# A GRU after a causal convolution on one core: the prologue's order of issue, and step 0's n part in a PSUM bank of its own

## The chip, the cores and the metric

The kernel runs on one core of a Trainium2 chip. The metric is the device time of one execution in microseconds (us), as the median of several runs. A profile is one further execution, whose span runs from its first to its last instruction.

## The reference

The input x has 16 rows (batch), 256 time steps and 512 channels; cond has 16 rows of 512. First a causal convolution over time with 16 taps in each channel, whose weights are the rows of cond, is added to x. Then a GRU cell runs over the 256 steps from the state h = cond, and its states are added to x.

```python
x = x + conv(x, w=cond_2048[:, None, :])     # depthwise, 16 taps, left padding of 15
def cell(h, x):
    gi = x @ W_ih + b_ih                     # [16, 1536]
    gh = h @ W_hh + b_hh
    i_r, i_z, i_n = split(gi, 3); h_r, h_z, h_n = split(gh, 3)
    r = sigmoid(i_r + h_r); z = sigmoid(i_z + h_z)
    n = tanh(i_n + r * h_n)
    return (1 - z) * n + z * h
x = x + scan(cell, h0=cond_2048, inputs=x)
```

All of it is in float32. The 256 steps depend on each other.

## The kernel before

The 512 channels lie as C = 4 chunks (c) of 128 on the partitions. A step is worked in H = 2 halves (f), each with two chunks of the output. A half's pre-activations stand in a PSUM bank `pg[m % 3][f]`, where m = t // 2 since a bank holds two steps at once; its 512 columns are split into the n part of the recurrence (columns 0 to 128), r and z (128 to 384) and the n part of the input (384 to 512). ScalarE first seeds a bank with the biases (`seed`, L430). Then TensorE adds the input's product (`product(q)`, L301: m, f and c are digits of q, and one q is four matmuls of 192 columns) and the recurrence's (`recur(t, f, c)`, L325, also four matmuls of 192). Every float32 matmul of these is two rows in the trace, so one `recur` or `product` is 8 rows, and a step is 64 rows of `recur` and 32 of `product`. The products of a step's round are for a later m; they are what TensorE does while the other engines turn the gates into the new state.

That chain runs once for each half: VectorE transposes r and z out of PSUM (L539) and n beside it (L543), ScalarE makes r and z (L461) and 1 - z (L463), VectorE scans n (L551), ScalarE takes the tanh (L466), GpSimd has z*h ready (L290), and VectorE scans the new h (L564). TensorE's next step waits for `s_h[0]`, and for `s_h[1]` after 24 of its rows.

Ahead of step 1 stands a **prologue**, written by hand and separately for each engine:

- SyncE queues the loads in one row: cnd (cond), xs (the first 16 steps of x), the four chunks of W_ih, the four of W_hh (`whh[:, c, F:]`, 768 KB each, L229). Then it waits for the third chunk of W_hh, loads `xb[1]`, and goes on with small loads (`tz`, `xw`) for the convolution of steps 16 to 47 on TensorE (`turn`, in steps 4, 6 and 9).
- ScalarE queues the two biases and, once GpSimd has made `cpad`, the store of the taps. It makes 16 diagonal matrices from cond (L446), seeds six banks, moves chunk 3 of x out of `pcv[0]` (L451), loads the table of the sigmoid (L452), and copies the n columns of each chunk of W_hh to the front of its row when the chunk has come (L455, 630 ns each). `recur` reads n, r and z as one strip of 192 columns, which needs that copy.
- TensorE zeroes the six banks of `pg` (L370), runs WARM = 6 matmuls on zeros (L372), the taps of chunk 3 (L364), the 16 products of m = 0 and 1, then step 0: chunk by chunk of W_hh, each with its wait, and with IDLE matmuls on zeros behind chunks 0 and 1. The last chunk is done by `recur_first` (L334), in matmuls of 128 and 64 columns, without the copy. Four products of m = 2 follow.
- VectorE copies cond into h, makes the biases (`bc`), then the convolution of chunks 0 to 2 for the first 16 steps: `first` and 48 pieces of `rest`. Before the last LATE = 22 of them stand the two transposes of the input's n part (`transpose_in`), for which step 0 waits.

## Time and profile before

| what | us |
|---|---|
| median of 3 runs | 1025.57 |
| lowest and highest | 1025.18, 1025.68 |
| the profiled execution | 1025.25 |
| its span | 1023.5 |
| TensorE busy with matmuls | 1015.4 |
| step 1's first matmul | 24.81 |
| from one step to the next, in steady state | 3.90 |

In the timeline rows the columns are start, time from the first start to the last end, engine, line, operation, tiles, shapes and count; in brackets the idle time of the engine before it and what ended it. PEld is TensorE's load of weights, ACTq and SPq the issue of DMAs. Most of the span is 255 steps of the same shape; the change touches what lies ahead of step 2.

### The profile page before, as it was taken

To read this page: it belongs to the slowest core of one execution; us is meant where nothing else is said; L and a number is where in the kernel's file an instruction comes from. 1 tells how busy PE (TensorE), PEld (TensorE's weight loads), DVE (VectorE), ACT (ScalarE), POOL (GpSimd) and SP (SyncE) were. 2 spreads that over 40 slices of the span, in tenths; PEclk is the share of its full clock that TensorE was granted. 3 is DMA by queue.
4 is the path that set the end of the run, shared out by engine and by line. 5 is a ranking of instruction groups with operands and counts; after the bars stand their busy time and mean duration, and the time that the engine had idled before them with its cause. 6 is when DMAs were issued, how large, how long until landed. Compare 5 with 4: busy or idle time off the path is not lost.

```text
span 1023.5 us, 58209 instructions
## 1 busy us (share of the span) xinstructions
PE 1015.4 (99%) x24837; PEld 902.6 (88%) x24838; DVE 865.1 (85%) x2851; ACT 399.3 (39%) x1816; POOL 237.4 (23%) x784
## 2 busy tenths in 40 slices
PE   8999999999999999999999999999999999999997
PEld 6988888888888888899999999999999999999986
DVE  7788888888888888888888888888888887777555
ACT  5334333333433343333434333343433333343333
POOL 3222222222222222222222222222222222222222
PEclk9999999999999999999999999999999999999999
DMA  8721001010100101001010010101001000000000
GB/s 297 73 34 39 19 21 30 15 36 19 29 25 12 34 19 34 23 12 35 15 39 19 15 36 11 39 19 29 22 14 35 14 29 16 11 29 4 24 14 12
DMA packets 66450, 32.07 MB, mean 31 GB/s; under 512 B 43920, under 2 KB 65040, under 8 KB 66192
## 3 DMA queue, kind: packets, MB, share of 16 engines
q1 hardware_dynamic: 65760, 28.25, 10.7%
q8 instruction: 195, 3.19, 1.3%
q14 instruction: 63, 0.52, 0.2%
q10 hardware_dynamic: 432, 0.11, 0.0%
HBM read 19.86 MB, written 8.49 MB: 28 GB/s over the span
## 4 chain that ended last, share of the span: by engine, by line
PE 97%; issue 1%; POOL 1%; DVE 0%; DMA 0%; ACT 0%; POOLq 0%; DVEq 0%
PE pg L328 65%; PE pg L318 32%; POOL tz L277 1%; PE pcv L356 0%; DMA cnd<-cond 0%; DVE hp L564 0%; POOL nzh L290 0%; DVE gt L539 0%; DVE gn L543 0%; ACT rz L461 0%; POOL cpad L267 0%; POOL nzh L274 0%; POOL rz L272 0%; POOL zcp L273 0%; POOL cpad L269 0%
## 5 line engine op out<-in xcount | busy, mean ns | idle before, releaser
L328 PE MATMUL pg<-whh,hp 128*32 128x192 f32 x16368 | 716.8, 326 | 2.1 <-ACT whh L455 1.1
L328 PEld LDWEIGHTS pg<-whh,hp 128*32 128x32 f32 x16368 | 594.3, 110 | 74.8 <-DVE hp L564 2.7
L318 PE MATMUL pg<-wih,x 128*32 128x192 f32 x8192 | 385.4, 326 | 0.0
L290 POOL TENSOR_TENSOR nzh<-rz,hp 128x32 f32<-128x32 f32 x512 | 158.0, 309 | 780.0 <-ACT rz L461 780.0
L318 PEld LDWEIGHTS pg<-wih,x 128*32 128x32 f32 x8192 | 296.5, 110 | 35.0
L461 ACT ACTIVATE rz<-gt 128x64 f32<-128x64 f32 x512 | 136.1, 266 | 484.6 <-DVE gt L539 459.1
L506 DVE SCALAR_TENSOR_TENSOR x<-xb,cnd,x 128x512 f32<-128x512 f32 (+1 forms) x420 | 294.6, 702 | 8.0
L564 DVE TENSOR_TENSOR_SCAN hp<-zcp,nzh 128x96 f32<-128x96 f32 x512 | 173.0, 338 | 41.4 <-ACT nzh L466 40.7
L539 DVE STREAM_TRANSPOSE gt<-pg 128x128 f32<-128x128 f32 x512 | 160.2, 313 | 50.8 <-PE pg L328 42.6
L551 DVE TENSOR_TENSOR_SCAN an<-rz,gn 128x64 f32<-128x64 f32 x512 | 148.7, 290 | 52.2 <-ACT rz L461 52.0
L466 ACT ACTIVATE nzh<-an 128x32 f32<-128x32 f32 x512 | 120.8, 236 | 125.6 <-DVE an L551 125.6
L463 ACT ACTIVATE zcp<-gt 128x32 f32<-128x32 f32 x512 | 111.0, 217 | 0.0
L543 DVE STREAM_TRANSPOSE gn<-pg 128x64 f32<-128x64 f32 x512 | 106.5, 208 | 0.0
L437 ACT ACTIVATE pg<-bc 128x256 f32<-128x256 f32 x256 | 86.4, 370 | 0.0
L284 POOL TENSOR_TENSOR x<-x,hp 128x64 f32<-128x64 f32 x255 | 81.5, 320 | 0.0
L534 DVE STREAM_TRANSPOSE gn<-pg 128x64 f32<-128x64 f32 x256 | 57.7, 226 | 0.1
L506 DVE SCALAR_TENSOR_TENSOR x<-xb,cnd 128x512 f32<-128x512 f32 (+1 forms) x28 | 19.3, 688 | 0.0
L490 DVE SCALAR_TENSOR_TENSOR x<-xs,cnd,x 128x192 f32<-128x192 f32 (+11 forms) x45 | 11.6, 335 | 0.0
L517 DVE SCALAR_TENSOR_TENSOR x<-xb,cnd,x 128x512 f32<-128x512 f32 x15 | 10.9, 727 | 0.2
L277 POOL MEMSET tz<- 128x2048 f32 x3 | 5.3, 1805 | 1.0 <-DVE bc L585 1.0
L455 ACT ACTIVATE whh<-whh 128x512 f32<-128x512 f32 x4 | 2.5, 630 | 7.1 <-DMA whh<-w_hh 7.1
L356 PEld LDWEIGHTS pcv<-tz,xw 128*32 128x32 f32 x192 | 5.0, 110 | 0.3
(47 smaller groups left out, 49.4 us busy)
## 6 DMA issues: line engine op xcount, KB each, us to landing
xb<-x SPq DMA_DIRECT2D x96, 94.0 KB, 2.0
out<-x SPq DMA_DIRECT2D x60, 128.0 KB, 1.9
wih<-w_ih SPq DMA_DIRECT2D x4, 768.0 KB, 8.0
whh<-w_hh SPq DMA_DIRECT2D x4, 768.0 KB, 14.2
xw<-x SPq DMA_DIRECT2D x24, 64.0 KB, 3.3
xb<-x SPq DMA_DIRECT2D x16, 62.0 KB, 1.8
tz<-taps SPq DMA_DIRECT2D x12, 64.0 KB, 3.5
xs<-x SPq DMA_DIRECT2D x1, 512.0 KB, 4.6
```

The lines of the kernel that those rows point to most:

```text
L290: pool.tensor_tensor(nzh[:, f, ::2, :, 1], chunks(rz[:, f, 1, :, 1]), h_of(t - 1, slice(f * CH, (f + 1) * CH)), ALU.mult).then_inc(s_zh[f], 1)
L318: i = pe.matmul(pg[m % Q][f][D * j:D * (j + 1), RZ:END], x1_of(c, 2 * m, 2 * m + 2), wih[:, c, :, :].rearrange("p (g k) (j d) -> p j g k d ...
L328: i = pe.matmul(pg[t // 2 % Q][f][D * j:D * (j + 1), 0:IN], hp[:, t % 2, 2 * c + 1 - t % 2:2 * c + 3 - t % 2, :, 1].rearrange("p u b -> p ...
L437: act.activation(pg[m % Q][f][:, 0:END], bc[:, f, :], ACT.Copy).then_inc(s_seed[f], 1)
L461: act.activation(rz[:, f, :, :, 1].rearrange("p g (c b) -> p (g c) b", b=B), gt[:, f, :, u], ACT.Sigmoid).then_inc(s_rz[f], 1)
L463: act.activation(zcp[:, f, ::2, :, 1], gt[:, f, CH:, u], ACT.Sigmoid, scale=-1.0).then_inc(s_zc[f], 1)
L466: act.activation(nzh[:, f, ::2, :, 0], chunks(an[:, f, :, 1]), ACT.Tanh).then_inc(s_n[f], 1)
L506: dve.scalar_tensor_tensor(o, xx[:, c, (K - 1 - lag) * B:(K - 1 - lag + n) * B], cnd[:, c, K - 1 - lag:K - lag], o if lag else now, ALU.mu ...
L539: dve.transpose(gt[:, f, :, :].rearrange("p c r -> p (c r)"), pg[t // 2 % Q][f][:, RZ:IN]).then_inc(s_trz[f], 1)
L543: dve.transpose(gn[:, t // 2 % 2, :, f, :, :, 0].rearrange("p u c b -> p c u b"), pg[t // 2 % Q][f][:, 0:RZ]).then_inc(s_tn[f], 1)
L551: dve.tensor_tensor_scan(an[:, f].rearrange("p n s -> p (n s)"), rz[:, f, 0].rearrange("p n s -> p (n s)"), gn[:, t // 2 % 2, t % 2, f].re ...
L564: dve.tensor_tensor_scan(hp[:, (t + 1) % 2, a:a + n].rearrange("p c b s -> p (c b s)"), zcp[:, f, 0:n].rearrange("p c b s -> p (c b s)"), ...
```

## The change

Step 0's recurrence for n goes to the bank `pcv[1]`, both halves side by side (`recur_n`), and r and z alone to `pg[0][f]` (`recur_rz`). So no chunk of step 0 needs ScalarE's copy, and the last chunk of W_hh is loaded in two DMAs, the r and z columns (512 KB, semaphore s_whh[3]) and then the n columns (256 KB, s_whl). ScalarE seeds `pcv[1]` with the biases (two activations of 128 columns), and TensorE zeroes one bank more. VectorE's `transpose_n` of step 0 waits for the new semaphore s_gn, which the last `recur_n` raises for both halves.

Order: cond is loaded by ScalarE's queue as its third DMA, no longer by SyncE's as its first. The sigmoid's table is loaded ahead of the diagonals by an activation on zeros. The store of the taps stands behind the fourth diagonal. On VectorE the biases come ahead of cond's copies, and LATE is 18. GpSimd's four memsets come ahead of its work on cond. Of the hunks left out below, one moves GpSimd's memsets and one VectorE's copies of cond; the others declare semaphores, or count the new waits. Three products of m = 2 are moved in between the chunks of W_hh, the chunk c = 3 of each half first, and step 0 has five instead of four, step 1 three instead of four. IDLE is 3 behind chunk 0 and 4 behind chunk 1.

```diff
@@ -30,8 +30,8 @@
 TAPS = 3 * K
 FEW = 4
 WARM = 6
-LATE = 22
-IDLE = {0: 5, 1: 3}
+LATE = 18
+IDLE = {0: 3, 1: 4}
 M2 = T // 2
 RZ, IN, END = CH * D, 3 * CH * D, 4 * CH * D
 Q = 3
...
@@ -154,7 +157,7 @@
             def until(t):
                 n = C * (t + 1) if t <= THIN else C * (THIN + 1) + (C - 1) * (t - THIN)
                 return 2 * H * C + min(n, H * C * (M2 - 2))
-            return range(until(t - 1), until(t))
+            return range(until(t - 1) + (t == 1), until(t))
 
         def inputs(t):
 
@@ -221,12 +224,13 @@
                 sp.wait_ge(s_o, b)
                 sp.dma_start(out[:, c, a * B:b * B], x1_of(c, a, b)).then_inc(s_out[k], 16)
 
-            sp.dma_start(cnd[:, :, :], cond).then_inc(s_cnd, 16)
             sp.dma_start(xs[:, :, :], x[:, :, 0:TB * B]).then_inc(s_xs, 16)
             for c in range(C):
                 sp.dma_start(wih[:, c, :, :], w_ih[:, c, :, :]).then_inc(s_wih[c], 16)
-            for c in range(C):
+            for c in range(C - 1):
                 sp.dma_start(whh[:, c, F:], w_hh[:, c, :]).then_inc(s_whh[c], 16)
+            sp.dma_start(whh[:, C - 1, F:3 * F], w_hh[:, C - 1, 0:2 * F]).then_inc(s_whh[C - 1], 16)
+            sp.dma_start(whh[:, C - 1, 3 * F:], w_hh[:, C - 1, 2 * F:]).then_inc(s_whl, 16)
             sp.wait_ge(s_whh[C - 2], 16)
             sp.dma_start(xb[1][:, 0, :], x[:, 0, B:(W2 + TB) * B]).then_inc(s_xe, 16)
             for t in range(T):
...
@@ -301,12 +305,15 @@
             def product(q):
 
                 m, f, c = q // (H * C), q // C % H, q % C
+                if m == 2:
+                    c = (c - 1) % C
                 if m < 2 and f == 0:
                     pe.wait_ge(s_wih[c], 16)
                 if m < 2 and c < C - 1:
                     pe.wait_ge(s_first, len(FIRST))
+                if q % C == 0:
+                    pe.wait_ge(s_seed[f], m + 1)
                 if c == 0:
-                    pe.wait_ge(s_seed[f], m + 1)
                     if FEW <= 2 * m < TB:
                         pe.wait_ge(s_first, len(FIRST) + len(REST))
                     elif TB <= 2 * m < LONG[0][0]:
@@ -319,7 +326,7 @@
                                   wih[:, c, :, :].rearrange("p (g k) (j d) -> p j g k d", g=3, j=J)
                                   [:, j, :, f * CH:(f + 1) * CH],
                                   start=False, stop=True, skip_group_check=True)
-                if c == C - 1:
+                if q % C == C - 1:
                     i.then_inc(s_gi[f], 1)
 
             def recur(t, f, c):
@@ -331,15 +338,20 @@
                                   start=False, stop=True, skip_group_check=True)
                 return i
 
-            def recur_first(f, c):
-
-                hh = hp[:, 0, 2 * c + 1:2 * c + 3, :, 1].rearrange("p u b -> p (u b)")
+            def recur_rz(f, c):
+
                 for j in range(J):
-                    o = pg[0][f][D * j:D * (j + 1), :]
-                    pe.matmul(o[:, RZ:IN], hh,
-                              whh[:, c, F:3 * F].rearrange("p (g j f n) -> p j f g n", g=2, j=J, f=H)[:, j, f],
-                              start=False, stop=True, skip_group_check=True)
-                    i = pe.matmul(o[:, 0:RZ], hh,
+                    i = pe.matmul(pg[0][f][D * j:D * (j + 1), RZ:IN],
+                                  hp[:, 0, 2 * c + 1:2 * c + 3, :, 1].rearrange("p u b -> p (u b)"),
+                                  whh[:, c, F:3 * F].rearrange("p (g j f n) -> p j f g n", g=2, j=J, f=H)[:, j, f],
+                                  start=False, stop=True, skip_group_check=True)
+                return i
+
+            def recur_n(f, c):
+
+                for j in range(J):
+                    i = pe.matmul(pcv[1][D * j:D * (j + 1), f * RZ:(f + 1) * RZ],
+                                  hp[:, 0, 2 * c + 1:2 * c + 3, :, 1].rearrange("p u b -> p (u b)"),
                                   whh[:, c, 3 * F:].rearrange("p (j f n) -> p j f n", j=J, f=H)[:, j, f],
                                   start=False, stop=True, skip_group_check=True)
                 return i
@@ -368,6 +380,7 @@
             for q in range(Q):
                 for f in range(H):
                     pe.matmul(pg[q][f][:, :], zeros[:, 0:P], zeros[:, :], start=True, stop=True).then_inc(s_bits, 1)
+            pe.matmul(pcv[1][:, :], zeros[:, 0:P], zeros[:, :], start=True, stop=True).then_inc(s_bits, 1)
             for _ in range(WARM):
                 pe.matmul(pcv[0][:, :], zeros[:, 0:P], zeros[:, :], start=True, stop=True)
             pe.wait_ge(s_xs, 16)
@@ -387,19 +400,25 @@
             pe.wait_ge(s_tin[1], 1)
             for f in range(H):
                 pe.wait_ge(s_h[f], 1)
-            for c in range(C):
+            pe.wait_ge(s_seed_n, H)
+            for c in range(C - 1):
                 pe.wait_ge(s_whh[c], 16)
-                if c < C - 1:
-                    pe.wait_ge(s_whn, c + 1)
                 for f in range(H):
-                    if c < C - 1:
-                        recur(0, f, c)
-                    else:
-                        recur_first(f, c).then_inc(s_gh[f], 1)
+                    recur_rz(f, c)
+                    recur_n(f, c)
+                if c < H:
+                    product((2 * H + c) * C)
                 for _ in range(IDLE.get(c, 0)):
                     pe.matmul(pcv[0][:, :], zeros[:, 0:P], zeros[:, :], start=True, stop=True)
-            for q in products(0):
-                product(q)
+            product(2 * H * C + 1)
+            pe.wait_ge(s_whh[C - 1], 16)
+            for f in range(H):
+                recur_rz(f, C - 1).then_inc(s_gh[f], 1)
+            pe.wait_ge(s_whl, 16)
+            recur_n(0, C - 1)
+            recur_n(1, C - 1).then_inc(s_gn, 1)
+            for c in range(1, C - 1):
+                product(2 * H * C + c + 1)
             pe.wait_ge(s_whn, C)
             for t in range(1, T):
                 m = t // 2
...
@@ -438,20 +457,25 @@
 
             act.dma_start(bih[:, :], b_ih).then_inc(s_small, 16)
             act.dma_start(bhh[:, :], b_hh).then_inc(s_small, 16)
-            act.wait_ge(s_cp, 3)
-            act.dma_start(scratch[:, :, :], cpad[:, :, :]).then_inc(s_scr, 16)
+            act.dma_start(cnd[:, :, :], cond).then_inc(s_cnd, 16)
+            act.wait_ge(s_clear, 1)
+            act.activation(pre[:, :], zeros[:, 0:B], ACT.Sigmoid)
             act.wait_ge(s_eye, 2)
             act.wait_ge(s_cnd, 16)
             for lag in range(K):
+                if lag == J:
+                    act.wait_ge(s_cp, 3)
+                    act.dma_start(scratch[:, :, :], cpad[:, :, :]).then_inc(s_scr, 16)
                 act.activation(diagonal(lag), eye[:, :], ACT.Copy, scale=cnd[:, C - 1, K - 1 - lag:K - lag]).then_inc(s_dg, 1)
             for m in range(Q):
                 for f in range(H):
                     seed(m, f)
+            for f in range(H):
+                act.activation(pcv[1][:, f * RZ:(f + 1) * RZ], bc[:, f, 0:RZ], ACT.Copy).then_inc(s_seed_n, 1)
             act.wait_ge(s_c3, 1)
             act.activation(x1[:, C - 1, 0:TB * B], pcv[0][:, 0:TB * B], ACT.Copy).then_inc(s_ev, 1)
-            act.activation(pre[:, :], cnd[:, 0, :], ACT.Sigmoid)
             for c in range(C):
-                act.wait_ge(s_whh[c], 16)
+                act.wait_ge(s_whh[c] if c < C - 1 else s_whl, 16)
                 act.activation(whh[:, c, 0:F], whh[:, c, 3 * F:], ACT.Copy).then_inc(s_whn, 1)
             act.wait_ge(s_zero, 4)
             for t in range(T):
@@ -540,8 +564,11 @@
                               pg[t // 2 % Q][f][:, RZ:IN]).then_inc(s_trz[f], 1)
 
             def transpose_n(t, f):
+                if t == 0:
+                    dve.wait_ge(s_gn, 1)
+                g = pg[t // 2 % Q][f][:, 0:RZ] if t else pcv[1][:, f * RZ:(f + 1) * RZ]
                 dve.transpose(gn[:, t // 2 % 2, :, f, :, :, 0].rearrange("p u c b -> p c u b"),
-                              pg[t // 2 % Q][f][:, 0:RZ]).then_inc(s_tn[f], 1)
+                              g).then_inc(s_tn[f], 1)
 
             def scan_n(t, f):
 
...
```

On TensorE, from the end of the 16 products (pg10, pg11) to step 1, this stood before (`s_whn` is ScalarE's copy, L318 a product, L400 an idle matmul):

```order
L328 MATMUL pg00<-whh,hp 32x192 [waits s_h1,s_whh0,s_h0,s_whn,s_tin1,s_tin0]
L328 MATMUL pg00<-whh,hp 32x192 x3
L328 MATMUL pg01<-whh,hp 32x192 x4
L400 MATMUL pcv0<-zeros 128x512 x5
L328 MATMUL pg00<-whh,hp 32x192 [waits s_whn,s_whh1]
L328 MATMUL pg00<-whh,hp 32x192 x3
L328 MATMUL pg01<-whh,hp 32x192 x4
L400 MATMUL pcv0<-zeros 128x512 x3
L328 MATMUL pg00<-whh,hp 32x192 [waits s_whn,s_whh2]
L328 MATMUL pg00<-whh,hp 32x192 x3
```

Now, from the chunk c = 2 on (L344 is r and z, L353 n, L325 a product, L412 an idle matmul):

```order
L344 MATMUL pg00<-whh,hp 32x128 [waits s_whh2]
L344 MATMUL pg00<-whh,hp 32x128 x3
L353 MATMUL pcv1<-whh,hp 32x64 x4
L344 MATMUL pg01<-whh,hp 32x128 x4
L353 MATMUL pcv1<-whh,hp 32x64 x4
L325 MATMUL pg20<-wih,x1 32x192 [waits s_first]
L325 MATMUL pg20<-wih,x1 32x192 x3
L344 MATMUL pg00<-whh,hp 32x128 [waits s_whh3]
L344 MATMUL pg00<-whh,hp 32x128 x3
L344 MATMUL pg01<-whh,hp 32x128 x4
L353 MATMUL pcv1<-whh,hp 32x64 [waits s_whl]
L353 MATMUL pcv1<-whh,hp 32x64 x7
```

The recurrence for n has left the bank of r and z, twice as many matmuls stand in each chunk, no wait for the copy is left, and a product has come ahead of the last chunk's wait. Two more stand ahead of this piece, behind the chunks c = 0 and 1.

On ScalarE, from the start to the first copy of W_hh, before:

```order
L439 DMA bih<-b_ih 128x12
L440 DMA bhh<-b_hh 128x12
L442 DMA taps<-cpad 128x192 [waits s_cp]
L446 ACT_TABLE_LOAD [waits s_cnd]
L446 ACTIVATE xb<-eye,cnd 128x128 [waits s_eye]
L446 ACTIVATE xb<-eye,cnd 128x128 x15
L437 ACTIVATE pg<-bc 128x256 [waits s_bc,s_bits] x6
L451 ACTIVATE x<-pcv 128x256 [waits s_c3]
L452 ACT_TABLE_LOAD
L452 ACTIVATE pre<-cnd 128x16
L455 ACTIVATE whh<-whh 128x512 [waits s_whh0]
```

and now:

```order
L458 DMA bih<-b_ih 128x12
L459 DMA bhh<-b_hh 128x12
L460 DMA cnd<-cond 128x64
L462 ACT_TABLE_LOAD
L462 ACTIVATE pre<-zeros 128x16 [waits s_clear]
L469 ACTIVATE xb<-eye,cnd 128x128 [waits s_cnd,s_eye]
L469 ACTIVATE xb<-eye,cnd 128x128 x3
L468 DMA taps<-cpad 128x192 [waits s_cp]
L469 ACTIVATE xb<-eye,cnd 128x128 x12
L456 ACTIVATE pg<-bc 128x256 [waits s_bc,s_bits] x6
L474 ACTIVATE pcv<-bc 128x64 x2
L476 ACTIVATE x<-pcv 128x256 [waits s_c3]
L479 ACTIVATE whh<-whh 128x512 [waits s_whh0]
```

One of the two table loads is gone, the other stands ahead of the wait for cond, and cond's own load is third in this engine's queue.

On VectorE in step 0, now (L563 is r and z, L570 n, L578 the scan of n, L591 that of h):

```order
L563 STREAM_TRANSPOSE gt<-pg00 128x128 [waits s_gh0]
L570 STREAM_TRANSPOSE gn<-pcv1 128x2x2x16 [waits s_gn]
L578 SCALAR_TENSOR_TENSOR an<-rz,gn 128x64 [waits s_tin0,s_tn0,s_rz0]
L563 STREAM_TRANSPOSE gt<-pg01 128x128 [waits s_gh1]
L570 STREAM_TRANSPOSE gn<-pcv1 128x2x2x16 [waits s_gn]
L591 SCALAR_TENSOR_TENSOR hp<-zcp,nzh 128x96 [waits s_zc0,s_zh0,s_n0]
```

The rows are those of before but for the wait for s_gn, and for pcv1 as what n is read from.

## Rows read from the trace of the kernel before

**Rows 1.** The page: busy time of each engine; the instruction queue (packets, MB, share).

```profile
PE 1015.4 (99%) x24837; PEld 902.6 (88%) x24838; DVE 865.1 (85%) x2851; ACT 399.3 (39%) x1816; POOL 237.4 (23%) x784
...
q8 instruction: 195, 3.19, 1.3%
```

**Rows 2.** Timeline of TensorE from 3.79 us to step 3.

```profile
3.79 2.67 PE L372 MATMUL pcv<-zeros 128*128 128x512 bf16 x6
...
16.53 0.86 PE L328 MATMUL pg<-whh,hp 128*32 128x192 f32 x16
...
19.38 0.86 PE L328 MATMUL pg<-whh,hp 128*32 128x192 f32 x16 [0.80 <-ACT whh L455]
20.16 0.82 PE L400 MATMUL pcv<-zeros 128*128 128x512 bf16 x3
...
22.35 0.45 PE L339 MATMUL pg<-whh,hp 128*32 128x128 f32 x8
...
23.07 1.49 PE L318 MATMUL pg<-wih,x 128*32 128x192 f32 x31
24.81 2.81 PE L328 MATMUL pg<-whh,hp 128*32 128x192 f32 x64 [0.24 <-DVE hp L564]
27.40 1.51 PE L318 MATMUL pg<-wih,x 128*32 128x192 f32 x32
28.70 2.81 PE L328 MATMUL pg<-whh,hp 128*32 128x192 f32 x64
```

**Rows 3.** Timeline of ScalarE in the prologue.

```profile
3.65 1.28 ACT L446 ACT_TABLE_LOAD   x1 [3.65 <-POOL cpad L269]
4.94 4.79 ACT L446 ACTIVATE xb<-eye,cnd 128x128 f32<-128x128 f32 x16
...
20.48 0.63 ACT L455 ACTIVATE whh<-whh 128x512 f32<-128x512 f32 x1 [1.25 <-DMA whh<-w_hh]
22.33 0.63 ACT L455 ACTIVATE whh<-whh 128x512 f32<-128x512 f32 x1 [1.22 <-DMA whh<-w_hh]
23.42 0.26 ACT L461 ACTIVATE rz<-gt 128x64 f32<-128x64 f32 x1 [0.46 <-DVE gt L539]
```

**Rows 4.** Timeline of VectorE: the convolution's start, step 0, step 1's first h.

```profile
5.87 0.68 DVE L480 SCALAR_TENSOR_TENSOR x<-xs,cnd 128x64 f32<-128x64 f32 x3 [0.88 <-DMA xs<-x]
...
16.06 0.37 DVE L534 STREAM_TRANSPOSE gn<-pg 128x64 f32<-128x64 f32 x2
16.36 4.42 DVE L490 SCALAR_TENSOR_TENSOR x<-xs,cnd,x 128x128 f32<-128x128 f32 x22
...
23.71 0.29 DVE L551 TENSOR_TENSOR_SCAN an<-rz,gn 128x64 f32<-128x64 f32 x1 [0.26 <-ACT rz L461]
...
24.30 0.36 DVE L564 TENSOR_TENSOR_SCAN hp<-zcp,nzh 128x96 f32<-128x96 f32 x1
...
28.05 0.31 DVE L564 TENSOR_TENSOR_SCAN hp<-zcp,nzh 128x96 f32<-128x96 f32 x1
```

**Rows 5.** Timeline of SyncE's queue: the first two loads.

```profile
0.81 0.39 SPq L224 DMA_DIRECT2D cnd<-cond  x1
1.25 0.68 SPq L225 DMA_DIRECT2D xs<-x  x1
```

**Rows 6.** DMA issues: queue, count, KB each, median us to landing.

```profile
taps<-cpad ACTq DMA_DIRECT2D x1, 96.0 KB, 7.3
cnd<-cond SPq DMA_DIRECT2D x1, 32.0 KB, 1.8
```

**Rows 7.** Stretches of 1 us: start:end, length, each engine's busy time, PEclk, DMA share, GB/s.

```profile
19.00:20.00 1.00, 0.62 (x16) 0.50 (x16) 1.00 (x7) 0.23 (x1) 0.00 (x0) 1.00 1.03 420
20.00:21.00 1.00, 0.99 (x11) 0.21 (x3) 0.78 (x6) 0.52 (x1) 0.00 (x0) 1.00 0.44 178
```

**Rows 8.** DMA queues by stretch, 16.0:17.3, then 22.4:24.0: packets, MB, share of 16 engines.

```profile
q8 instruction: 1, 0.02, 4.6%
...
q8 instruction: 1, 0.02, 4.4%
```

More of the change, by code:

```diff
@@ L91, in build @@
         s_whh = [sem(f"s_whh{c}") for c in range(C)]
+        s_whl = sem("s_whl")
         s_whn = sem("s_whn")
@@ L114, in build @@
         s_x1 = sem("s_x1")
+        s_seed_n = sem("s_seed_n")
         s_seed = halves("s_seed")
@@ L117, in build @@
         s_tin = halves("s_tin")
+        s_gn = sem("s_gn")
         s_gh = halves("s_gh")
@@ L264, in _ @@
                                channel_multiplier=1).then_inc(s_eye, 1)
+            pool.memset(an[:, :, :, :], 0.0).then_inc(s_zero, 1)
+            pool.memset(rz[:, :, :, :, :], 0.0).then_inc(s_zero, 1)
+            pool.memset(zcp[:, :, :, :, :], 0.0).then_inc(s_zero, 1)
+            pool.memset(nzh[:, :, :, :, :], 0.0).then_inc(s_zero, 1)
             pool.wait_ge(s_cnd, 16)
@@ L270, in _ @@
                                ALU.add).then_inc(s_cp, 1)
-            pool.memset(an[:, :, :, :], 0.0).then_inc(s_zero, 1)
-            pool.memset(rz[:, :, :, :, :], 0.0).then_inc(s_zero, 1)
-            pool.memset(zcp[:, :, :, :, :], 0.0).then_inc(s_zero, 1)
-            pool.memset(nzh[:, :, :, :, :], 0.0).then_inc(s_zero, 1)
             pool.wait_ge(s_bc, H)
@@ L432, in seed @@
                 if m < Q:
-                    act.wait_ge(s_bits, 2 * Q)
+                    act.wait_ge(s_bits, 2 * Q + 1)
                     act.wait_ge(s_bc, H)
@@ L570, in _ @@
             dve.memset(hp[:, :, :, :, :], 0.0).then_inc(s_clear, 1)
-            dve.wait_ge(s_cnd, 16)
-            dve.wait_ge(s_clear, 2)
-            for f in range(H):
-                dve.tensor_copy(h_of(-1, slice(f * CH, (f + 1) * CH)),
-                                cnd[:, f * CH:(f + 1) * CH, :]).then_inc(s_h[f], 1)
             dve.wait_ge(s_small, 32)
@@ L587, in _ @@
                               ).then_inc(s_bc, 1)
+            dve.wait_ge(s_cnd, 16)
+            dve.wait_ge(s_clear, 2)
+            for f in range(H):
+                dve.tensor_copy(h_of(-1, slice(f * CH, (f + 1) * CH)),
+                                cnd[:, f * CH:(f + 1) * CH, :]).then_inc(s_h[f], 1)
             dve.wait_ge(s_xs, 16)
```

## The prediction

> **What bounds the kernel now.** The page first: TensorE is busy for 1015.4 of 1023.5 us [rows 1]. The timeline of TensorE shows where that comes from: step 1 starts at 24.81 and step 2 at 28.70, 3.89 us later, with no idle time between the 64 rows of the recurrence and the 32 of products [rows 2]. From step 1 almost to the end the time is a count of matmuls, and 255 steps times 3.9 us are there whatever the prologue does. Whatever moves step 1's start moves the end by as much, as long as no later step has to wait. So the question is what releases step 1, and the timelines of the other engines up to 24.81 answer it, read backwards. Step 1 waits for h: its scan ends at 24.30 + 0.36 = 24.66, and the matmul comes 0.15 later. That scan follows the scan of n at 23.71 by 0.59 [rows 4]. The scan of n waits for r at 23.42 + 0.26 = 23.68 on ScalarE [rows 3], r for VectorE's transpose and that for the last chunk of W_hh, whose matmuls start at 22.35 [rows 2]. They start with the landing: ScalarE's copy of the same chunk starts at 22.33, after an idle 1.22 that a DMA ended, and the copy of the chunk before at 20.48, likewise [rows 3]. The chain of the prologue is a stream of loads, then 2.48 us of work.
>
> **The loads.** SyncE issues cond at 0.81 and xs at 1.25 [rows 5]. With cond gone from its queue, xs and the eight weights behind it start 0.44 earlier. All 16 engines of the DMA are full up to 20 us (share 1.03) [rows 7], so the stream is bound by bytes, and the bytes are the same. I take 0.44 for the landings; the ends are 0 (the start was not what set them) and 0.44. The n columns, now the last load, then land at 22.33 - 0.44 = 21.89. The r and z columns are two thirds of a chunk that takes 22.33 - 20.48 = 1.85, so they land 0.62 before that, at 21.27.
>
> **The chain behind the last load.** ScalarE's copy of the last chunk still stands ahead of the first r, and it now waits for the n columns. It runs from 21.89 for 0.63 to 22.52 [rows 3]. TensorE and VectorE work beside it. The last chunk took TensorE 23.07 - 22.35 = 0.72 [rows 2]; r and z, two thirds, can be done from 21.27 on, and VectorE can transpose them before the copy ends. So r starts at the copy's end instead of 23.42: 22.54 to 22.80, and the scan of n 0.03 later at 22.83. The n part needs a third of 0.72 after 21.89, some 0.1 of latency, and a transpose of about 0.2, which ends at 22.45 and is hidden under the copy. Gain: 23.71 - 22.83 = 0.88, half of it from the stream, half from taking matmuls and a transpose out of the chain.
>
> **Is TensorE there in time?** Its path ahead of that is new. VectorE's transposes for step 0 started at 16.06, and LATE puts four more pieces ahead of them; the 22 that followed took 0.20 each, and the first are the longest [rows 4], so I take 0.25 each: 16.06 - 0.44 + 1.0 + 0.37 = 17.0. TensorE's own work ended at 16.53, and one more zeroing matmul costs (6.29 - 3.79) / 6 = 0.42, which gives 16.95, the same [rows 2]. From 17.0: three chunks of 0.72, three products of 8 rows (1.30 / 4 = 0.33 each), seven idle matmuls of 0.22 to 0.27 (three of them took 0.82 to the end of the last [rows 2]), at 0.22, make 4.7, so it reaches the r and z part of the last chunk at 21.7, 0.4 after it has landed. It is through at 21.7 + 0.72 = 22.4, and the scan of n could come at 22.8 by this path. The two paths are equal within the 0.2 us that I can't resolve; the copy's wait for TensorE in chunk 1, 0.80 idle [rows 2], is gone and has been filled with products. I count no loss, and 0.3 as the far end.
>
> **Step 1 has 24 rows of products.** That is 8 times 1.30 / 32 = 0.33 less [rows 2]. But step 2 waits for h, ready at 28.05 + 0.31 = 28.36 and usable 0.15 later, at 28.51, where it started at 28.70 [rows 2, 4]. The gain is 0.19, and the chain is late next; from step 2 on a step has 32 rows again and covers it. The bounds are 0 and 0.33. The product that left step 1 runs ahead of the last chunk, under the wait for loads.
>
> **At nothing.** The table load (1.28, from 3.65) and the diagonals behind it (4.79) [rows 3] are off the path: one load remains and runs before cond is there, the diagonals may start earlier, but TensorE takes them only from 6.7 on. ScalarE's two new seeds and the store of the taps lie in its pause before the first copy. SyncE's queue behind the weights moves earlier with them.
>
> **Sum.** 0.88 + 0.19 = 1.07 us. Against the profiled execution, 1025.25 - 1.07 = 1024.18; that execution is 0.32 under the median, so 1024.5 for the median.
>
> **Rival 1: a fetch of instructions lands on the last load.** The share of the DMA falls from 1.03 to 0.44 between 20 and 21 us, yet the last chunk lands only at 22.33 [rows 3, 7]. Most DMA engines are done and a few are late. Between 16.0 and 17.3 a packet of the instruction queue held 4.6% of 16 engines, 0.046 x 16 x 1.3 = 0.96 us of one engine, and the next came after 22.4, when the weights were in [rows 8]. TensorE's 24,837 matmuls and 24,838 loads of weights over 195 packets are 255 instructions to a packet [rows 1]. Behind the 16 products, 240 instructions led through the last product before; now the doubled matmuls and the moved products make 238 by the end of chunk 2, at about 21.2. So the second packet falls at about 21, with the last load still running. If it goes to the engine that is late already, n lands up to 0.96 later, at 22.85, the copy follows, and the scan of n comes at 23.79: 0.08 lost, 0.19 gained, 1025.45; half a hit gives 1025.0. Against it: no row says which engine fetches, and 0.4 us decide whether the packet still meets the load. The Trainium skill (Runtime: NRT & Kernel Launch, Instruction fetch mechanics) says that a sequencer refills in blocks of 256 instructions over its own DMA queue and that crossing a block is mostly hidden. The trace agrees on the size; by "mostly hidden" this rival would be nothing and the time 1024.5, and no row here tells what a block does to a load beside it.
>
> **Rival 2, the slower side: cond lands late.** It is now ScalarE's third DMA, behind xs and the first weights; with a DMA each 0.44, as SyncE's first two stand [rows 5], it is issued at 0.81 + 0.88 = 1.7. The nearest rows are cond alone, 1.8 us to landing, and the taps on the same queue among the weights, 7.3 us [rows 6]: it lands between 3.5 and 9.0. VectorE started its convolution at 5.87, when xs had come [rows 4]; that is 5.43 now, and with the two copies of h ahead (0.32) it needs cond by 5.1. Each microsecond beyond moves VectorE's convolution, hence its transposes, TensorE's step 0 and the end. At 6.15 the whole gain is gone; at 9.0 the loss is 3.9 - 1.07 = 2.83, and the time 1028.4. I take 4.2, near the cond row: it is a third of the taps' bytes, and it runs beside xs, where the taps met the full stream of weights. The Trainium skill (DMA: Bandwidth & Descriptors, Queues, rings and completion order) says that each DMA engine takes turns between its queues packet by packet; by that a short load does not stand behind the weights, which would give 1024.5 too. The 7.3 us of the taps show that taking turns can be slow.
>
> **How the numbers follow.** Forecast 0.46, 1024.5. Rival 1 0.33, 1025.0 to 1025.5. Rival 2 0.09, of which 0.04 beyond 8.2 us, where it costs more than 2 us. Waits that open in later steps, up to 0.5 us (SyncE's queue for the turns starts only 0.44 earlier, TensorE 1.07), 0.05. A larger gain than summed, by a stream that starts still earlier, 0.07. The range from 1023.9 to 1025.9 takes in the first, rival 1, the later waits and the mild part of rival 2; it leaves out about 0.13. A change of less than 0.2%, 2.05 us, is not told from none by a measurement of this kernel, and every likely case lies within: faster 0.03, same 0.93, slower 0.04.
>
> **What would show it.** Step 1's first matmul at 23.9, the scan of n at 22.8, ScalarE's last copy at 21.9, step 2 3.7 us after step 1. Rival 1: the last copy past 22.4 with r and z's matmuls near 21.7, and the instruction packet before 21.9. Rival 2: the diagonals start after 5.1. Later waits: idle time ahead of the turns in steps 4, 6 and 9. The forecast is wrong if ScalarE's last copy starts no earlier than 22.33, or if idle time opens in the steps behind.

## The result, and the profile after

| | before | after |
|---|---|---|
| median of 12 executions each, us | 1025.51 | 1027.78 |
| lowest to highest, us | 1025.18 to 1025.89 | 1027.60 to 1028.34 |
| profiled execution, us | 1025.25 | 1028.33 |
| its span, us | 1023.5 | 1026.6 |

The ratio of after to before is 1.0023, with a 95% interval of 1.0015 to 1.0030. The change made the kernel slower by 2.27 us; 1024.5 was forecast, and 1027.78 lies above the range. The profiled execution of after is 0.55 above its median, so the trace shows 3.08 us of difference where the medians show 2.27. Of the executions reported below, one ran at a granted clock of 0.56 from start to end and took 1803 us (the first of the kernel with six more matmuls ahead); it is left out, and its trace was not used.

The page of after: the busy time of TensorE, and the lines of the chain that ended last.

```profile
PE 1017.0 (99%) x24885; PEld 867.7 (85%) x24886; DVE 865.6 (84%) x2851; ACT 399.6 (39%) x1817; POOL 238.6 (23%) x784
...
PE pg L335 65%; PE pg L325 32%; DMA cnd<-cond 1%; PE pcv L376 1%; PE pcv L368 0%; PE pg L344 0%; PE pcv L412 0%; PE pcv L353 0%; DVE hp L591 0%; DVE gt L563 0%; DVE gn L570 0%; ACTq L459 0%; ACT xb L469 0%; ACTq L458 0%; POOL nzh L294 0%
```

The last line names what is new: the load of cond stands in the chain with 1% of 1026.6 us. The timelines show it. ScalarE in after (start, length, instruction, in brackets the idle time before it and what ended it), and the time from the issue of cond to its landing:

```profile
1.71 0.53 ACTq L460 DMA_DIRECT2D cnd<-cond  x1
...
8.71 0.69 ACT L469 ACTIVATE xb<-eye,cnd 128x128 f32<-128x128 f32 x2 [4.94 <-DMA cnd<-cond]
...
19.30 0.63 ACT L479 ACTIVATE whh<-whh 128x512 f32<-128x512 f32 x1 [1.27 <-DMA whh<-w_hh]
22.33 0.63 ACT L479 ACTIVATE whh<-whh 128x512 f32<-128x512 f32 x1 [2.39 <-DMA whh<-w_hh]
```
```profile
DMA to landing us min/median/max: 6.9/6.9/6.9
```

VectorE in after, from the copies of h to the transposes for step 0:

```profile
8.65 0.31 DVE L613 COPY hp<-cnd 128x32 f32<-128x32 f32 x2 [2.51 <-DMA cnd<-cond]
8.88 0.67 DVE L504 SCALAR_TENSOR_TENSOR x<-xs,cnd 128x64 f32<-128x64 f32 x3
...
20.06 0.46 DVE L558 STREAM_TRANSPOSE gn<-pg 128x64 f32<-128x64 f32 x2
```

TensorE in after, from the taps to step 2:

```profile
9.17 6.35 PE L376 MATMUL pcv<-xs,xb 128*128 128x256 f32 x32 [1.91 <-ACT xb L469]
15.44 5.41 PE L325 MATMUL pg<-wih,x 128*32 128x192 f32 x128
20.67 0.40 PE L344 MATMUL pg<-whh,hp 128*32 128x128 f32 x8
...
25.63 0.62 PE L344 MATMUL pg<-whh,hp 128*32 128x128 f32 x16
...
28.07 2.81 PE L335 MATMUL pg<-whh,hp 128*32 128x192 f32 x64 [0.95 <-DVE hp L591]
...
31.77 1.51 PE L335 MATMUL pg<-whh,hp 128*32 128x192 f32 x32
```

Read against before. The convolution starts 8.88 - 5.87 = 3.01 later [rows 4]. VectorE's transposes for step 0 start 20.06 - 16.06 = 4.00 later: those 3.01, and 1.0 for the four pieces put ahead of them. Step 1 starts 28.07 - 24.81 = 3.26 later, step 2 31.77 - 28.70 = 3.07 later [rows 2], and that is the whole difference of the spans, 3.1. Nothing is lost or won behind step 2. The last load of W_hh lands at 22.33, as in before [rows 3], but TensorE comes to the last chunk only at 25.63: in after the loads don't bound the prologue, cond does.

How TensorE took this: from 7.26 to 9.17 it had nothing to do, and the granted clock (the figure ahead of DMA share and GB/s) fell from its upper level, 2.4 GHz, to 1.2 GHz, and came back during the next stretch:

```profile
10.00:12.00 2.00, 2.00 (x7) 1.83 (x6) 2.00 (x11) 2.00 (x8) 2.00 (x2) 0.50 0.99 412
12.00:14.00 2.00, 2.00 (x12) 2.00 (x12) 2.00 (x7) 2.00 (x8) 2.00 (x2) 0.66 1.05 420
```

So there were two candidates for the loss beside each other, VectorE's late convolution and TensorE's slow taps, both behind one landing; and one question on the landing: why 6.9 us, where the same 32 KB took 1.8 in before [rows 6]?

### The profile page after: what moved, and what is told of

It reads as the page before. It is cut to its first block, busy times and chain, and to the rows that moved or that the text cites. A ratio compares the mean times of both kernels' runs of the same rounds, so it can differ in the third digit from the quotient of the medians.

```text
span 1026.6 us, 58303 instructions
## 1 busy us (share of the span) xinstructions
PE 1017.0 (99%) x24885; PEld 867.7 (85%) x24886; DVE 865.6 (84%) x2851; ACT 399.6 (39%) x1817; POOL 238.6 (23%) x784
## 4 chain that ended last, share of the span: by engine, by line
PE 98%; DMA 1%; DVE 0%; issue 0%; ACTq 0%; ACT 0%; POOL 0%; POOLq 0%; DVEq 0%
PE pg L335 65%; PE pg L325 32%; DMA cnd<-cond 1%; PE pcv L376 1%; PE pcv L368 0%; PE pg L344 0%; PE pcv L412 0%; PE pcv L353 0%; DVE hp L591 0%; DVE gt L563 0%; DVE gn L570 0%; ACTq L459 0%; ACT xb L469 0%; ACTq L458 0%; POOL nzh L294 0%
## 5 line engine op out<-in xcount | busy, mean ns | idle before, releaser
L335 PEld LDWEIGHTS pg<-whh,hp 128*32 128x32 f32 x16320 | 568.3, 110 | 97.6 <-DVE hp L591 2.8
L325 PE MATMUL pg<-wih,x 128*32 128x192 f32 x8192 | 384.4, 326 | 0.0
L325 PEld LDWEIGHTS pg<-wih,x 128*32 128x32 f32 x8192 | 284.1, 110 | 46.9
L591 DVE TENSOR_TENSOR_SCAN hp<-zcp,nzh 128x96 f32<-128x96 f32 x512 | 173.3, 339 | 41.8 <-ACT nzh L490 41.2
L563 DVE STREAM_TRANSPOSE gt<-pg 128x128 f32<-128x128 f32 x512 | 160.3, 313 | 49.9 <-PE pg L335 42.4
L578 DVE TENSOR_TENSOR_SCAN an<-rz,gn 128x64 f32<-128x64 f32 x512 | 149.4, 292 | 51.6 <-ACT rz L485 51.3
L570 DVE STREAM_TRANSPOSE gn<-pg 128x64 f32<-128x64 f32 x510 | 106.4, 209 | 0.0
L376 PE MATMUL pcv<-xs,xb 128*128 128x256 f32 (+15 forms) x32 | 6.3, 369 | 1.9 <-ACT xb L469 1.9
L376 PEld LDWEIGHTS pcv<-xs,xb 128*128 128x128 f32 x32 | 6.0, 237 | 2.5 <-ACT xb L469 2.3
L469 ACT ACTIVATE xb<-eye,cnd 128x128 f32<-128x128 f32 x16 | 4.8, 388 | 4.9 <-DMA cnd<-cond 4.9
```

The lines of the kernel that those rows point to most:

```text
L325: i = pe.matmul(pg[m % Q][f][D * j:D * (j + 1), RZ:END], x1_of(c, 2 * m, 2 * m + 2), wih[:, c, :, :].rearrange("p (g k) (j d) -> p j g k d ...
L335: i = pe.matmul(pg[t // 2 % Q][f][D * j:D * (j + 1), 0:IN], hp[:, t % 2, 2 * c + 1 - t % 2:2 * c + 3 - t % 2, :, 1].rearrange("p u b -> p ...
L563: dve.transpose(gt[:, f, :, :].rearrange("p c r -> p (c r)"), pg[t // 2 % Q][f][:, RZ:IN]).then_inc(s_trz[f], 1)
L570: dve.transpose(gn[:, t // 2 % 2, :, f, :, :, 0].rearrange("p u c b -> p c u b"), g).then_inc(s_tn[f], 1)
L578: dve.tensor_tensor_scan(an[:, f].rearrange("p n s -> p (n s)"), rz[:, f, 0].rearrange("p n s -> p (n s)"), gn[:, t // 2 % 2, t % 2, f].re ...
L591: dve.tensor_tensor_scan(hp[:, (t + 1) % 2, a:a + n].rearrange("p c b s -> p (c b s)"), zcp[:, f, 0:n].rearrange("p c b s -> p (c b s)"), ...
```

## The experiments

Theory: cond's late landing is the whole loss, and it is late because its packets take turns with SyncE's full queue. Rivals: the prologue's new order costs by itself (TensorE later at the last chunk, the instruction packet); the fallen clock sets the end; cond is late because of its place in ScalarE's own queue.

**cond back on SyncE's queue, the rest of the change kept.**

```diff
+            sp.dma_start(cnd[:, :, :], cond).then_inc(s_cnd, 16)
             sp.dma_start(xs[:, :, :], x[:, :, 0:TB * B]).then_inc(s_xs, 16)
...
             act.dma_start(bhh[:, :], b_hh).then_inc(s_small, 16)
-            act.dma_start(cnd[:, :, :], cond).then_inc(s_cnd, 16)
```

> The changed kernel with cond's load back as SyncE's first DMA (xs second again, at 1.25) and nothing else undone. Theory (cond's landing at 8.6 us on ScalarE's queue is the whole loss): cond lands at 2.6, the convolution starts at 5.9 with xs, VectorE's transposes for step 0 end at 17.4, the clock does not fall, and the last copy starts at 22.3; the scan of n comes at 23.3 and step 1 at 24.4, so 1024.9 us. Rival A (the instruction packet hits the last load): the n columns land a microsecond late, the last copy starts near 23.3, step 1 at 25.3, 1025.9 us. Rival B (the doubled matmuls or the new waits cost by themselves): step 1 after 25.5 with the loads in time, above 1026.2.

Measured: 1025.13 us (median of 10), ratio 0.9997 (0.9987 to 1.0007). The one line takes back 1027.78 - 1025.13 = 2.65 us, the whole loss. What it leaves is no loss, but also not the gain of the sum. TensorE, ScalarE's last copy and VectorE's scan of n in this kernel:

```profile
17.40 0.43 PE L345 MATMUL pg<-whh,hp 128*32 128x128 f32 x8 [0.26 <-DVE gn L558]
...
18.53 0.82 PE L413 MATMUL pcv<-zeros 128*128 128x512 bf16 x3
19.28 0.43 PE L345 MATMUL pg<-whh,hp 128*32 128x128 f32 x8
...
20.41 1.04 PE L413 MATMUL pcv<-zeros 128*128 128x512 bf16 x4
21.38 0.43 PE L345 MATMUL pg<-whh,hp 128*32 128x128 f32 x8
...
22.39 0.62 PE L345 MATMUL pg<-whh,hp 128*32 128x128 f32 x16
...
24.83 2.81 PE L336 MATMUL pg<-whh,hp 128*32 128x192 f32 x64 [0.95 <-DVE hp L591]
...
28.53 0.70 PE L336 MATMUL pg<-whh,hp 128*32 128x192 f32 x12
```
```profile
22.33 0.63 ACT L479 ACTIVATE whh<-whh 128x512 f32<-128x512 f32 x1 [1.26 <-DMA whh<-w_hh]
```
```profile
23.64 0.39 DVE L578 TENSOR_TENSOR_SCAN an<-rz,gn 128x64 f32<-128x64 f32 x1
```

Step 1 starts at 24.83, where before has 24.81. The scan of n is expected 0.94 after the landing, at 23.3, and comes at 23.64, because the last chunk's r and z start at 22.39, when both loads are already in. TensorE is late, not the loads: it starts step 0 at 17.40, and its seven idle matmuls cost 0.75 + 0.97 us. Step 2 follows step 1 by 28.53 - 24.83 = 3.70, where before has 3.89: the term for the 24 rows holds, to the second digit.

**cond third on ScalarE's queue, in the kernel before, alone.**

```diff
-            sp.dma_start(cnd[:, :, :], cond).then_inc(s_cnd, 16)
             sp.dma_start(xs[:, :, :], x[:, :, 0:TB * B]).then_inc(s_xs, 16)
...
             act.dma_start(bhh[:, :], b_hh).then_inc(s_small, 16)
+            act.dma_start(cnd[:, :, :], cond).then_inc(s_cnd, 16)
```

> The kernel before with one part of the change alone: cond's load moved from SyncE's first to ScalarE's third DMA. Theory: cond lands at about 8.6; the diagonals wait for it and for the table load behind it, the clock falls to its lower level while TensorE waits for the first diagonal, TensorE starts step 0 near 22 and step 1 comes 3 to 4 us late, 1028.5 to 1029.5. Rival (the late cond is an effect of the other edits, of the order of the loads on SyncE's queue for instance): cond lands before 5 and the time stays at 1025.5.

Measured: 1029.57 us (median of 4), ratio 1.0041 (1.0027 to 1.0056). VectorE's first use of cond, ScalarE's diagonals, and TensorE's taps and step 1 (this execution, the profiled one, took 1030.77, 1.2 above the median):

```profile
9.04 0.31 DVE L574 COPY hp<-cnd 128x32 f32<-128x32 f32 x2 [7.24 <-DMA cnd<-cond]
```
```profile
11.41 4.79 ACT L446 ACTIVATE xb<-eye,cnd 128x128 f32<-128x128 f32 x16
```
```profile
11.86 6.61 PE L363 MATMUL pcv<-xs,xb 128*128 128x256 f32 x32 [5.28 <-ACT xb L446]
...
30.23 1.02 PE L327 MATMUL pg<-whh,hp 128*32 128x192 f32 x20 [0.24 <-DVE hp L564]
```

The move alone costs 4.0 us, and cond is late without any other part of the change. In before's order the store of the taps, which waits for GpSimd's work on cond, and the table load (1.28) both stand between cond and the diagonals, so these start at 11.41 instead of 8.71, and here VectorE's transposes for step 0 wait 2.39 us for TensorE. It is likely, and not tried by itself, that the new order on ScalarE, which the forecast put at nothing, is why after loses 1.8 us less than this kernel.

**cond first on ScalarE's queue, the biases after 18 pieces of VectorE's convolution.**

```diff
+            act.dma_start(cnd[:, :, :], cond).then_inc(s_cnd, 16)
             act.dma_start(bih[:, :], b_ih).then_inc(s_small, 16)
             act.dma_start(bhh[:, :], b_hh).then_inc(s_small, 16)
-            act.dma_start(cnd[:, :, :], cond).then_inc(s_cnd, 16)
...
+            dve.wait_ge(s_xs, 16)
+            for q in range(len(FIRST)):
+                first(q)
+            for q in range(6):
+                rest(q)
             dve.wait_ge(s_small, 32)
...
-            for q in range(len(REST) - LATE):
+            for q in range(6, len(REST) - LATE):
```

The copies of h go ahead of the convolution with it.

> The changed kernel with cond as ScalarE's first DMA, ahead of the biases, xs still SyncE's first; VectorE copies cond into h and does the first 18 pieces of its convolution before it makes the biases. Theory: a short load is late by its place behind xs and the weights, so cond lands at about 2.6 here and the stream of weights still starts 0.44 earlier; last copy at 21.9, step 1 at 23.9, 1024.4. If the instruction packet hits the last load: the last copy at 22.9 and 1025.4. Rival (ScalarE's queue is slow whatever the place): cond lands after 5 again and the time is over 1026. The biases are then late instead and should cost nothing before 10 us.

Measured: 1025.64 us (median of 10), ratio 1.0004 (0.9994 to 1.0013). The profiled execution took 1026.32, as two more of the ten took over 1026.5, so its trace shows some 0.7 us more than the median. VectorE:

```profile
2.51 0.31 DVE L601 COPY hp<-cnd 128x32 f32<-128x32 f32 x2 [0.71 <-DMA cnd<-cond]
5.19 0.68 DVE L504 SCALAR_TENSOR_TENSOR x<-xs,cnd 128x64 f32<-128x64 f32 x3 [2.37 <-DMA xs<-x]
...
17.45 0.38 DVE L558 STREAM_TRANSPOSE gn<-pg 128x64 f32<-128x64 f32 x2
```

cond is in 1.7 us after its issue, and xs 0.68 earlier than in before (5.19 against 5.87). But the last load of W_hh lands at 22.16, only 0.17 earlier than 22.33, and the biases, with their transposes 1.1 us of VectorE's time (9.22 to 10.33), push step 0's transposes to 17.45. TensorE starts step 0 at 17.93 and is at the last r and z at 22.91, and no gain is left. The first load in ScalarE's queue is fast even with xs issued on SyncE's at the same time. What freeing SyncE's first place brings to the weights, one trace can't tell: the last load's landing differs by more than 0.3 us between traces of the same order of loads (below).

**SyncE waits for cond before it loads xs.** cond is third in ScalarE's queue, as in after, but SyncE's queue is empty meanwhile.

```diff
+            sp.wait_ge(s_cnd, 16)
             sp.dma_start(xs[:, :, :], x[:, :, 0:TB * B]).then_inc(s_xs, 16)
```

> The changed kernel, where SyncE waits for cond's landing before it issues xs and the weights; cond stays ScalarE's third DMA. Theory (cond's packets take turns with the large packets of SyncE's queue, and so do the biases' ahead of them): with SyncE silent cond lands at 3.5 to 4.0 us instead of 8.6. Rival (ScalarE's third DMA is slow by its place in its own queue): it lands at 8 again. The time itself says nothing here: the weights start some 3 us late, and step 1 near 27.5.

Measured: 1027.83 us (one execution), and from the issue of cond to its landing:

```profile
DMA to landing us min/median/max: 1.9/1.9/1.9
```

Same queue, same place, 1.9 us instead of 6.9. The place alone doesn't slow cond; SyncE's packets do, once it comes behind the biases. (The time is no better, since now xs comes 2.8 later; step 1 starts at 27.60.) How it happens is in the rows of the DMA queues; q1 is SyncE's, q10 ScalarE's. First before from 2.0 to 3.0 us, then after from 3.0 to 4.0 and from 6.0 to 7.0:

```profile
q10 hardware_dynamic: 263, 0.01, 16.6%
```
```profile
q10 hardware_dynamic: 104, 0.00, 8.8%
```
```profile
q1 hardware_dynamic: 68, 0.34, 88.2%
q10 hardware_dynamic: 66, 0.02, 7.3%
```

In before the packets of the biases go through by themselves, before xs has begun. In after xs is issued 0.45 earlier, at 0.80, and they are still under way from 3 to 5 us; those of cond, 128 packets in the same queue behind them, go from 4.7 to 8.1. The row of 6.0 to 7.0 has 68 packets of one queue and 66 of the other: turns, as the Trainium skill (DMA: Bandwidth & Descriptors, Queues, rings and completion order) has it. But each turn costs the small load the time of a large packet, 0.882 x 16 / 68 = 0.21 us. Turns of one and one are not the whole account: from 5 to 6 us SyncE's queue moved 52 packets and ScalarE's 25, and from 2.3 to 3.0 153 and 2; why, no row says.

The biases, only 12 KB, are 256 packets ahead of cond's 128, and it is their number that holds cond back, not their bytes. The third experiment's trace shows it: b_hh is the third load there, also behind 256 packets and issued at 1.7, and its own 128 packets carry 6 KB where cond's carry 32. Its time from issue to landing, then ScalarE's queue from 6.0 to 7.0 us (b_hh) and from 8.0 to 9.0 (mostly the taps):

```profile
DMA to landing us min/median/max: 6.5/6.5/6.5
```
```profile
q10 hardware_dynamic: 67, 0.00, 4.2%
```
```profile
q10 hardware_dynamic: 67, 0.05, 15.1%
```

A fifth of the bytes, and nearly the same time; and 67 packets in a microsecond, whatever they carry, beside 67 and 68 of SyncE's.

**Six more matmuls to fill TensorE's idle time** (WARM from 6 to 12), in two runs.

> The changed kernel with WARM = 12: six more matmuls on zeros fill TensorE's wait for the first diagonal, so the clock should not fall to its lower level at 10 to 13 us. Theory (VectorE's late convolution sets step 0, the clock only rides along): the taps are 1.8 us shorter, but VectorE's transposes for step 0 still end at 20.5, and the time falls by 0.2 at most, to 1027.6. Rival (the fallen clock is the loss): TensorE's 16 products end 1.8 us earlier and the time falls by 1.5 or more, to 1026.3.

> The kernel of e4_warm_longer once more, for a trace at the usual clock. Theory (VectorE's late convolution sets step 0, the fallen clock only rides along): TensorE is granted the full clock from 10 to 13 us, its products end some 1.5 us before 20.8, and it then waits for VectorE's transposes at 20.5; step 1 starts at 27.9 or 28.0, as in the changed kernel. Rival (TensorE at the lower clock set it): step 1 starts before 27.5.

Measured: 1027.90 us (median of nine), ratio 1.0023 (1.0014 to 1.0033). The second run is one execution, 1028.44 us, 0.54 above that median, as after's profiled one is 0.55 above its own. Its granted clock, then TensorE:

```profile
10.00:12.00 2.00, 2.00 (x15) 2.00 (x14) 2.00 (x10) 2.00 (x8) 2.00 (x2) 1.00 1.03 430
```
```profile
9.06 4.78 PE L376 MATMUL pcv<-xs,xb 128*128 128x256 f32 x32 [1.27 <-ACT xb L469]
...
20.43 0.43 PE L344 MATMUL pg<-whh,hp 128*32 128x128 f32 x8 [1.21 <-DVE gn L558]
...
28.14 2.16 PE L335 MATMUL pg<-whh,hp 128*32 128x192 f32 x48 [0.96 <-DVE hp L591]
```

The clock stays at its upper level, the taps take 4.78 instead of 6.35, and TensorE then waits 1.21 us for VectorE's transposes. Step 0 starts at 20.43 instead of 20.67, step 1 at 28.14 instead of 28.07, and the medians, 1027.90 and 1027.78, are the same. The fallen clock cost nothing here; VectorE's late convolution set the end.

**The idle matmuls of chunk 0 and one of chunk 1 taken out, with cond on SyncE** (IDLE from {0: 3, 1: 4} to {1: 3}).

> The changed kernel with cond back on SyncE, and of the idle matmuls of step 0 only three, behind chunk 1. Theory (there TensorE sets step 1: step 0 began at 17.4 and the matmuls on zeros and the moved product brought it to the last chunk at 22.4, 0.7 after r and z had landed): TensorE reaches r and z at 21.7, the last copy still starts at 22.3, and r of step 0 follows it; scan of n at 23.3 instead of 23.64, step 1 at 24.5, 0.37 less than with all seven idle matmuls, 1024.8. Rival (the loads or the copy already set it): unchanged at 1025.1. Against the idle matmuls' purpose: if the granted clock falls between 18 and 24 us it is slower than 1025.5.

Measured: 1024.80 us (median of 10), ratio 0.9994 (0.9985 to 1.0003), 0.33 below the same kernel with seven. The intervals here are some 0.9 us to either side, so this step, and the next two, rest on the traces and not on the medians. TensorE's last n part and step 1:

```profile
22.68 0.43 PE L354 MATMUL pcv<-whh,hp 128*32 128x64 f32 x16
...
24.61 2.81 PE L336 MATMUL pg<-whh,hp 128*32 128x192 f32 x64 [0.85 <-DVE hp L591]
```

TensorE reaches the last chunk at 22.04 instead of 22.39. The last load landed at 22.66 in this execution, and step 1 starts 24.61 - 22.66 = 1.95 later; with seven idle matmuls it was 24.83 - 22.33 = 2.50. TensorE had been late, not the loads. The granted clock stays at 1.00 from 18 to 24 us without them.

**The last copy behind step 0's activations, on top of that.** The copy of the last chunk's columns, which the forecast took to set r, leaves the chain; TensorE waits for it only before the last chunk of step 1.

```diff
-            pe.wait_ge(s_whn, C)
+            pe.wait_ge(s_whn, C - 1)
...
+                if t == 1:
+                    pe.wait_ge(s_whn, C)
                 recur(t, 0, 3).then_inc(s_gh[0], 1)
...
+                if t == 0:
+                    act.wait_ge(s_whl, 16)
+                    act.activation(whh[:, C - 1, 0:F], whh[:, C - 1, 3 * F:], ACT.Copy).then_inc(s_whn, 1)
```

> The kernel with fewer idle matmuls, and the copy of the last chunk moved behind ScalarE's six activations of step 0; TensorE waits for it in step 1 only before it uses that chunk. Theory: the copy is then off the chain, and the n part sets it: n's columns land at 22.3, matmuls to 22.75, transpose to 23.06, scan of n at 23.15, step 1 at 24.3, 1024.6. Rival (the wait on the n columns, not the copy, had been the bound all along): no change against the run with fewer idle matmuls.

Measured: 1024.82 us (median of 10), ratio 0.9994 (0.9984 to 1.0003). TensorE:

```profile
22.31 0.43 PE L354 MATMUL pcv<-whh,hp 128*32 128x64 f32 x16
...
24.24 2.81 PE L336 MATMUL pg<-whh,hp 128*32 128x192 f32 x64 [0.85 <-DVE hp L596]
```

From the n part to step 1 it is 1.93 us with the copy in the chain (24.61 - 22.68) and 1.93 without it (24.24 - 22.31). Taking the copy out of the chain gained nothing, where 0.2 had been expected. That the two traces stand 0.37 apart is due to the loads, which landed that much apart in these two executions; the medians are 0.02 apart.

**Without the bank of its own for n, on top of that.** n's recurrence of step 0 goes into the same bank as r and z, so VectorE reads r and z only when n is written too. (A half's n part is 64 columns wide, so both took 128 of `pcv[1]`; ScalarE seeded them with two activations of 64 columns each.)

```diff
-                    i = pe.matmul(pcv[1][D * j:D * (j + 1), f * RZ:(f + 1) * RZ],
+                    i = pe.matmul(pg[0][f][D * j:D * (j + 1), 0:RZ],
...
-                recur_rz(f, C - 1).then_inc(s_gh[f], 1)
+                recur_rz(f, C - 1)
             pe.wait_ge(s_whl, 16)
-            recur_n(0, C - 1)
-            recur_n(1, C - 1).then_inc(s_gn, 1)
+            for f in range(H):
+                recur_n(f, C - 1).then_inc(s_gh[f], 1)
```

> As the one with the copy behind, but step 0's n part goes back to the bank of r and z; VectorE's transposes wait for the whole bank. This prices the bank of its own alone. Theory: r and z can no longer be transposed beside the last matmuls; they come at 22.7 to 23.0, r at 23.3, the scan of n at 23.35 instead of 23.15, so 0.2 more, 1024.8. Rival (the own bank is worth the whole 0.5 us of matmul and transpose that it takes out of the chain): 1025.1.

Measured: 1025.03 us (median of 10), ratio 0.9996 (0.9987 to 1.0006), 0.21 above the kernel with the bank. In the trace the n part starts at 22.86 and step 1 at 25.05, 2.19 apart instead of 1.93: 0.26. Both say what the bank of its own is worth, a little over 0.2 us. A difference of 0.2 us between the medians would not be enough for this alone; that one trace of each has the same size in a stretch of 2 us is what carries it.

**cond first on ScalarE's queue, four more pieces late, three idle matmuls.** The kernel of the third experiment with LATE from 18 to 22, so that step 0's transposes come ahead of four more pieces, and IDLE as above.

> The version with cond first on ScalarE's queue, with LATE = 22 as before the change and three idle matmuls only, behind chunk 1. Theory: there VectorE's biases had pushed step 0 to 17.9 and the idle matmuls had pushed TensorE to the last chunk at 22.9, though the loads had landed 0.2 earlier than with cond on SyncE; with both taken back the loads set step 1 again, 1.93 after the n columns land at 22.1 to 22.2: 24.1, 1024.6, 1.0 less than that version and about 0.2 less than the kernel with fewer idle matmuls and cond on SyncE (1024.8). Rival (the loads' start doesn't matter, what is gained ahead is lost again under the small packets): 1024.8 to 1025.0.

Measured: 1024.52 us (median of 11), ratio 0.9990 (0.9981 to 0.9999). It beats both kernels, before by 0.98 us, which is just clear of the interval, and after by 3.26. VectorE around step 0, then TensorE:

```profile
22.60 0.25 DVE L570 STREAM_TRANSPOSE gn<-pcv 128x64 f32<-128x64 f32 x1 [0.18 <-PE pcv L353]
22.94 0.29 DVE L578 TENSOR_TENSOR_SCAN an<-rz,gn 128x64 f32<-128x64 f32 x1
```
```profile
16.99 0.43 PE L344 MATMUL pg<-whh,hp 128*32 128x128 f32 x8 [0.44 <-DVE gn L558]
...
21.64 0.62 PE L344 MATMUL pg<-whh,hp 128*32 128x128 f32 x16
22.10 0.43 PE L353 MATMUL pcv<-whh,hp 128*32 128x64 f32 x16
...
24.04 2.81 PE L335 MATMUL pg<-whh,hp 128*32 128x192 f32 x64 [0.85 <-DVE hp L591]
```

TensorE starts step 0 at 16.99 and is at the last r and z at 21.64, the two times that the prediction had for the changed kernel (17.0 and 21.7), though with four fewer idle matmuls and four fewer pieces ahead. Now the last load bounds again, as the forecast wanted it, and step 1 starts 0.77 earlier than in before. With 0.19 for the 24 rows that makes 0.96; the medians have 0.98.

## Why the prediction was wrong, step by step

**The landing of cond is the step that failed.** "I take 4.2, near the cond row: it is a third of the taps' bytes, and it runs beside xs, where the taps met the full stream of weights" gave between 3.5 and 9.0 the wrong end: 8.6 was measured. Neither reason held. Behind the biases cond's packets began only at 4.7 us, when xs was nearly through, and met the full stream like the taps; and what counts are packets, not bytes. The row of the taps, 7.3 us, was the nearer one: the same queue beside the same stream. The rest of this rival held. It needed cond by 5.1, so the loss is 8.6 - 5.1 - 1.07 = 2.4, and the time 1028.0; 1027.78 was measured. That the two agree to 0.2 is in part luck: the 8.6 was read in an execution 0.55 above the median, and of the 1.07 that the sum takes off only 1025.55 - 1025.13 = 0.42 was there with cond early. The mechanism had been named and priced, and was given a chance of 0.09, of which 0.04 for a landing this late. The choice of the row decided, not the arithmetic.

**The start of the stream, 0.44:** neither shown nor refuted. With SyncE starting on xs the last load of W_hh was in at 22.33 (after), 21.98 (six more matmuls), 22.16 and 22.08 (cond first on ScalarE's queue), 22.14 in the mean. With cond ahead of xs it was in at 22.33 in before and in the first experiment, at 22.66 with fewer idle matmuls, and, by TensorE's n part, near 22.3 and 22.8 in the two kernels after that, 22.5 in the mean. The means are about 0.35 apart, but each group is spread over 0.3 to 0.5, so these traces can't tell 0.44 from 0.2 or from 0. After itself shows ScalarE's last copy at 22.33, the forecast's own sign of being wrong; the same kernel with six more matmuls ahead shows it at 21.98.

**The chain behind the last load, 0.44:** about the right size, by another way. From the last landing to step 1 before has 24.81 - 22.33 = 2.48, and the kernels with three idle matmuls 1.95 and 1.96 (24.04 - 22.08), a gain of 0.5. The prediction let the copy set r; moving it away changed nothing, 1.93 us both times. What sets the end is the n part: its matmuls, transpose, scan. Where TensorE is there in time, the scan of n comes 0.86 after the landing (22.94 - 22.08); the prediction had 0.94. The bank of its own is worth 0.21 to 0.26 of the gain.

**TensorE in time:** mis-sized by 0.7 us. 21.7 was worked out, 22.39 measured with cond landing early. The idle matmuls cost 0.25 each and not 0.22 (0.2 in all), and step 0 started at 17.40 and not 17.0, with the transposes at 16.94 behind a convolution that had not moved ahead. "I count no loss, and 0.3 as the far end" was too little. With cond back on SyncE the stream's half of the 0.88 is given back by the edit, and this ate the other half: step 1 at 24.83, where the loads alone would have had it near 24.4. So with cond early the change comes to 1025.1, inside the range, and still without the forecast gain.

**24 rows in step 1, 0.19:** right, 3.70 us from step 1 to step 2 in after and in each experiment on it with cond early, 3.89 in before.

**Rival 1, the instruction packet on the last load:** it came a little earlier than worked out (about 21) and did no harm. With cond on SyncE a packet of the instruction queue fell at 20.26, while the last load ran (the stretch from 20.0 to 21.3):

```profile
q1 hardware_dynamic: 114, 0.21, 42.4%
q8 instruction: 1, 0.02, 4.9%
```

0.049 x 16 x 1.3 = 1.02 us of one engine, yet the last copy starts at 22.33, 1.89 behind the one before (1.85 in before). So it held up none of the packets that landed last; on which engine it went no row says. That agrees with "mostly hidden" of the Trainium skill (Runtime: NRT & Kernel Launch, Instruction fetch mechanics); the packet ahead of it does not (below).

**"Later waits":** none. All of after's difference is there at step 2.
